# Filter stage of a four-layer graph network: second bias added by TensorE, product taken straight from PSUM

## What is computed

```python
row, col = (ei[0], ei[1])
filt = silu(rbf @ Wf1 + bf1) @ Wf2 + bf2      # 50000 x 256
msg = x[col] * filt
agg = segment_sum(msg, row, num_segments=N)
h = silu(agg @ Wu1 + bu1) @ Wu2 + bu2
```

## Time and profile before

| | us |
|---|---|
| median of 3 runs | 8960.01 (8955.36 to 8965.50) |
| profiled execution | 8954.23 |
| its span | 8952.5 |
| filter stage within the span, first to last scatter-add issue | 6350.6 to 7707.9 |
| POOL busy in the span | 5545.9 (62%) |
| DVE busy in the span | 6238.9 (70%) |
| PE busy in the span | 4724.6 (53%) |

### The profile page before, as it was taken

How to read it: one execution, slowest core, us unless ns; L and a number is a source line. 1 busy time by engine, 2 the same in 40 slices (tenths; PEclk the granted TensorE clock), 3 DMA queues, 4 the chain that set the end, 5 groups by cost and what they waited for, 6 DMA issues and landing times. The chain is left out here.

```text
span 8952.5 us, 103278 instructions
## 1 busy us (share of the span) xinstructions
PE 4724.6 (53%) x18908; PEld 3435.4 (38%) x18908; DVE 6238.9 (70%) x20123; ACT 3276.4 (37%) x8442; POOL 5545.9 (62%) x5121
## 2 busy tenths in 40 slices
PE   8855000019998333337771111100588888799944
PEld 4422000018886211225551111100455555688833
DVE  7899333348887999988987777799544444455577
ACT  4533001337776111117870000144322222244499
POOL 7877777765554666657767777677788888300000
PEclk9999555559998555559995555555677777899955
DMA  0299899989997444549994444599544444566699
GB/s 21 82 345 345 287 304 301 308 281 303 303 302 235 147 146 148 147 133 313 337 310 119 122 123 122 156 273 269 130 79 79 79 79 79 131 202 202 192 342 345
DMA packets 1143019, 1839.84 MB, mean 206 GB/s; under 512 B 218094, under 2 KB 564898, under 8 KB 1142374
## 3 DMA queue, kind: packets, MB, share of 16 engines
q1 hardware_dynamic: 637094, 927.78, 31.4%
q0 software_dynamic: 257536, 587.44, 25.7%
q10 hardware_dynamic: 247744, 318.00, 10.4%
HBM read 1044.55 MB, written 788.03 MB: 205 GB/s over the span
## 5 line engine op out<-in xcount | busy, mean ns | idle before, releaser
L701 POOL DMA_INDIRECT st<-S,last_i x1176 | 1421.0, 1208 | 650.3 <-issue 316.4
L915 POOL DMA_INDIRECT rows<-T,src_i x784 | 802.6, 1024 | 251.0 <-issue 248.6
L642 ACT ACTIVATE xo<-z,shift,rsd 128x256 f32<-128x256 f32 x1568 | 854.7, 597 | 4.4 <-issue 4.4
L1128 POOL DMA_INDIRECT A<-comb,ai x392 | 702.6, 1792 | 159.2 <-issue 143.9
L931 PE MATMUL psE<-encs,attr 4*128 4x256 f32 x784 | 404.8, 668 | 743.3 <-DMA attr<-in_attr3T 743.3
L946 ACT ACTIVATE ex<-diff 128x32 f32<-128x32 f32 x392 | 89.9, 229 | 1711.7 <-DVE diff L993 1711.7
L1200 DVE TENSOR_SCALAR eq<-psI,src_f 128x128 f32<-128x128 f32 x392 | 136.8, 349 | 742.6 <-DMA A<-comb,ai 708.7
L931 PE MATMUL psE<-fes,attr 64*128 64x8 f32 x784 | 199.5, 363 | 823.0 <-DMA attr<-in_attr64T 820.7
L477 DVE SCALAR_TENSOR_TENSOR sums<-sums,same,rows 128x256 f32<-128x256 f32 x784 | 380.7, 486 | 322.3 <-ACT rows L458 308.0
L1142 PE MATMUL psH<-rbf,wf1s 20*128 20x256 f32 x784 | 279.9, 486 | 600.2 <-DMA rbf<-in_rbfT 600.2
L931 PEld LDWEIGHTS psE<-encs,attr 4*128 4x128 f32 x784 | 227.4, 319 | 920.4 <-DMA attr<-in_attr3T 882.7
(11 more groups left out here) (232 smaller groups left out, 15603.8 us busy)
## 6 DMA issues: line engine op xcount, KB each, us to landing
X<-xo ACTq DMA_DIRECT2D x588, 256.0 KB
xt<-X SPq DMA_DIRECT2D x588, 256.0 KB
S<-sums SPq DMA_DIRECT2D x392, 272.0 KB, 2.4
A<-zero SPq DMA_DIRECT2D x392, 256.0 KB, 4.7
S<-sums SPq DMA_DIRECT2D x392, 256.0 KB, 4.1
xt<-in_x SPq DMA_DIRECT2D x392, 256.0 KB
T<-tt ACTq DMA_DIRECT2D x196, 280.0 KB
T<-tt ACTq DMA_DIRECT2D x196, 272.0 KB
```

The source lines that it names most:

```text
L642: ins = e.activation(y[s][:, k, :], z[s][:, k, :], ACT.Identity, bias=shift[s][:, k, :], scale=rsd[s][:, k, :])
L701: e.indirect_dma_start(st[s][:, k, :], None, sums_table, bass.IndirectOffsetOnAxis(ap=last_i[:, c:c + 1], axis=0))\
L915: e.indirect_dma_start(rows[s][:, k, :], None, table, bass.IndirectOffsetOnAxis(ap=src_i[:, c:c + 1], axis=0))\
L1128: e.indirect_dma_start(A[k], bass.IndirectOffsetOnAxis(ap=ai[s][:, k, :], axis=0), comb[s][:, k, :], None, compute_op=ALU.add).then_inc(si ...
```

## The change

The second bias is no longer added by VectorE. TensorE adds it into the same PSUM accumulation, as a matmul of a row of 128 ones by the bias row, once per column of a step. VectorE then multiplies psF by the gathered rows in one instruction instead of two, with no wait between. A tile of ones is filled once in `setup`.

```diff
+        one_row = sb("one_row", [1, P])
...
+                        e.memset(one_row[:], 1.0)
...
                             for k in range(G):
                                 for m in range(K):
-                                    mm = e.matmul(psF[s % 2][:, k * D:(k + 1) * D], hid[s][:, m, k * P:(k + 1) * P], wf2s[:, m, :],
-                                                  start=m == 0, stop=m == K - 1)
+                                    e.matmul(psF[s % 2][:, k * D:(k + 1) * D], hid[s][:, m, k * P:(k + 1) * P], wf2s[:, m, :],
+                                             start=m == 0, stop=False)
+                                mm = e.matmul(psF[s % 2][:, k * D:(k + 1) * D], one_row[:], bf2s[0:1, :], start=False, stop=True)
                             mm.then_inc(signal(filtered, s), 1)
...
-                            e.tensor_tensor(fl[s][:], psF[s % 2][:].rearrange("p (g d) -> p g d", g=G),
-                                            bf2s[:].rearrange("p (g d) -> p g d", g=1).to_broadcast([P, G, D]), ALU.add).then_inc(msteps, 1)
-                            e.wait_ge(msteps, i * NS + (s + 1))
-                            e.tensor_tensor(fl[s][:], fl[s][:], rows[s][:], ALU.mult).then_inc(signal(message, s), 1)
+                            e.tensor_tensor(fl[s][:], psF[s % 2][:].rearrange("p (g d) -> p g d", g=G), rows[s][:], ALU.mult).then_inc(signal(message, s), 1)
```

## The result

The changed kernel takes 9686.31 us (median of 4 runs, 9681.26 to 9694.75) against 8962.76 us for the kernel before, measured beside it. The ratio is 1.0808 (95% interval 1.0795 to 1.0821): 8.1% slower, where 0.8% faster was forecast.

What follows compares the result with a forecast made beforehand. It took POOL's scatter-add loop, with the landing last, to bound the filter stage: 8954.2 - 71.6 + 1 = 8883.6 us, and 5.8 more for the median, so 8889 us, range 8862 to 8920.

Steps and rivals of the forecast that it cites:

- POOL's loop: Filter stage: scatter-adds, landing, next step; removing L1220's stall of 0.38 us in 188 of 196 steps gains 71.6 us.
- The rival that denied it: Filter stage: the 1.98 us scatter-add is not due to L1220, or another VectorE instruction replaces it; 8960 us, chance 0.08.
- The one that let the landing come sooner: Filter stage: stall goes and landing comes sooner, so POOL's own 6.43 us bounds the step; 8855 us median, chance 0.07.
- 6.61: Filter stage: forecast step in us without the stall, 1.62 + 0.30 + 1.60 + 2.41 + 0.68, against 6.99 stalled.
- a fixed 2.41 us: Filter stage: distance from the second scatter-add's end to its landing, read as the same in two steps.
- VectorE's saved 141 us: VectorE in the filter stage: one instruction and gap fewer per step, 196 x 0.72 us, worth nothing by itself before a wait.
- the price of the added matmuls: TensorE, filter stage: two one-row matmuls per step cost 0.95 us at full clock, 1.8 at half, up to 1.13 and 2.07.
- My step of 8.1 us: TensorE, filter stage: half-clock step before the change, 5.90 us plus an estimated 2.2 for `join`; 9.9 with the change.
- I expect the clock to rise as the gaps fill: TensorE, filter stage: clock rises from 0.78 as the 2.3 us gap shrinks to about 1; 0.8 or more expected.
- rival 1: Filter stage: TensorE, gapless at a low or falling clock, becomes the bound; at 0.70 +71 us, 9031 us, chance 0.09.
- The slack: TensorE at half clock: `filt` ends 5 us before the product needing it starts, against 1.8 us of added delay.

## Why the prediction was wrong, step by step

**Right: POOL's loop.** That the second scatter-add is held up by L1220's two SBUF inputs, that the landing passes this on in full, and that it is worth about 72 us: six variants have it, with a stage of 1282.1 to 1289.8 us against 1355.6. The rival that denied it (no effect of L1220) falls with the variant that keeps the sum in PSUM. The one that let the landing come sooner was not seen: the step is 6.57, not 6.43. That it is not 6.61 either is a small misreading. The landing is not a fixed 2.41 us behind the second scatter-add, as two steps had made it seem: over the stage's middle it varies from 2.2 to 2.8 us, with a mean of 2.37 in the kernel before and in the variant without the bias alike, and 1.62 + 0.30 + 1.59 + 2.37 + 0.68 = 6.56.

**Right: VectorE's saved 141 us are worth nothing by themselves.** The variant with the old two instructions has the changed kernel's stage to the tenth of a us. Where POOL's loop bounds it is nearly the same: with the sum in PSUM VectorE keeps both instructions and the stage is 1289.8 us, against 1282.3 with one.

**Wrong: the price of the added matmuls.** I took 0.95 us per step at the upper clock and 1.8 at the lower, from the spacing of full-height instructions that follow each other. A one-row pair takes 0.63 and 1.15 us, so four instructions take 1.26 and 2.30. The two columns between them take longer too, at the lower clock 1.84 + 2.01 = 3.85 us, where they took 3.42 (6995.93 to 6999.35 in the earlier trace rows). The sum is 2.7 us where I had 1.8. (My step of 8.1 us had 0.2 too much in it, from an estimate of 2.2 for a `join` that takes 2.01.) The row was there: four 20-row instructions at 2.07 us in the earlier trace rows, which the prediction named as the upper end and set aside. With the steps as measured, 5.66 us at the upper clock and 10.63 at the lower, an unchanged clock of 0.78 gives 0.56 / 5.66 + 0.44 / 10.63 = 0.140 steps per us, a step of 7.13, longer than today's 6.94. By this estimate the mis-sized term alone would have turned the sign (0.19 x 196 = +37 us).

**Wrong, and the larger part: "I expect the clock to rise as the gaps fill".** The gaps filled and the clock fell, from 0.78 to 0.50. Of the 3.66 us by which the step grew (10.60 against 6.94), 0.19 are what 7.13 would have cost, and about 3.5 are the clock. I had looked at how busy TensorE is and at its gaps, not at what it is busy with. The runs show that the height of the added instructions decides here which way the clock moves: 0.50, 0.65 and 0.94 for 1, 64 and 128 rows in the same place, 0.95 for 128 rows with nonzero weights in one, and 0.84 with nothing added and the stall gone. The Trainium skill, page "TensorE: Matmul & The Clock Gate", section "Why this matters for your kernels", gives the advice to keep TensorE busy continuously to reach the full clock; this case does not agree, with 1000.00 us busy of 1000 at 0.50.

**Wrong: how far rival 1 can go.** The mechanism was named (TensorE without a gap at a clock that stays low), but priced at a clock of 0.70, 9031 us, with a chance of 0.09. The lower level of the clock is 0.50, the kernel before was at it in nearly half of its steps, and such a step left POOL's loop behind even by my own figures (9.9 against 6.6 us). At 0.50 these give 196 x (9.9 - 6.94) = +580 us, 9540; with the measured 10.63 it is +723, and 724 were measured. The range left this end out.

**The slack was beside the point.** That the slow `filt` ends 5 us ahead of the product that reads it holds for one slow step between fast ones. Where every step is 10.6 us and the others need 6.6, any slack is used up after a few steps.

What stays open: what exactly is counted for the clock; what sets off a fall from its upper level; why one-row work in one piece ahead of the second layer leaves it where it was (0.84) and in two pieces between or around it pulls it down (0.50, 0.66); and the single run of 9718 us of the variant with full-height rows in the changed kernel's places.

## What to carry to other kernels

Where TensorE's clock moves between its levels in a stage, price added matmuls at the lower level in every step, and compare that with the loop that bounds now: if it is longer, a stage can lock into it, and slack between steps does not help. Where a matmul of few rows is only a vehicle for a bias, give it the full height (the bias row in all partitions, and weights of 1/128, or of one in the first row and zero below) and keep it out of the middle of full-height work. Each worked here alone, and both together, though one of the four runs with the full height in the middle took 9718 us. And look first whether the gain has a cheaper source: here it came from taking one SBUF input away from a VectorE instruction in front of GpSimd's indirect DMAs, which a sum left in PSUM does without any matmul.

## What the runs showed of the hardware that I had not expected

- The rows of the added matmuls change the clock itself: 0.50, 0.65, 0.94 for 1, 64, 128 rows, 0.84 without them. It is so between 1 and 64 rows though the durations are equal (a pair 0.63 us at the upper clock, 1.15 at the lower).
- Rows with zero weights count as rows: 0.95 with nonzero weights in one row of 128 (the bias passed through all of them).
- A low-height instruction among full-height ones costs more than its columns: 0.63 against 0.43 us for a pair at the upper clock, 1.15 against 0.86 at the lower. The weight load stands idle where the height changes ([0.65 <-issue] at 7013.50 in the changed kernel, behind a one-row pair).
- TensorE can be busy for all of 1800 us at half clock, and the same pattern of instructions can run at 1.00 for 65 us in one part of a stage and at 0.50 in the rest.
- A VectorE instruction with two SBUF inputs that starts 0.16 us ahead of the issue of an indirect DMA of GpSimd makes that DMA's issue 0.39 us longer; with one input in PSUM it does nothing (1.98 against 1.59 us).
